# One-hot of slot numbers laid out contiguous per choice, slot number repeated along its columns, and the table of Silu loaded ahead

## The reference, cut to what matters

```python
x = x + tanh(g_xattn[0]) * sliding_window_attention(layernorm(x), ctx, ctx)
# layer 0: 32 experts, 8 a token, out of 4 of 8 groups
scores = sigmoid(flat @ gate_w.T)
topk_w, topk_i = group_topk(scores)
for e in range(32):
    h = silu(flat @ wg[e].T) * (flat @ wu[e].T)
    acc = acc + w[:, e] * (h @ wd[e].T)          # w is 0 where e isn't chosen
x = x + tanh(g_ffn[0]) * (acc + shared(flat))
x = x + tanh(g_xattn[1]) * cross_attention(layernorm(x), ctx)
# layer 1: 8 experts of 256, 2 a token, and two shared ones
x = x + tanh(g_ffn[1]) * moe1(layernorm(x))
```

## Time and profile before

| | us |
|---|---|
| median of 3 timed runs | 1098.48 |
| lowest, highest | 1097.58, 1100.46 |
| profiled execution | 1091.63 |
| its span | 1089.8 |

### The profile page before, as it was taken

How to read it: one execution, slowest core, us unless ns; L and a number is a source line. 1 busy time by engine, 2 the same in 40 slices (tenths; PEclk the granted TensorE clock), 3 DMA queues, 4 the chain that set the end, 5 groups by cost and what they waited for, 6 DMA issues and landing times.

```text
span 1089.8 us, 20602 instructions
## 1 busy us (share of the span) xinstructions
PE 929.6 (85%) x5529; PEld 716.2 (66%) x5529; DVE 690.3 (63%) x1965; ACT 441.1 (40%) x1030; POOL 544.2 (50%) x581
## 2 busy tenths in 40 slices
PE   3468888887699999999999926979999998999893
PEld 3357777776545888888888614655656564787672
DVE  5669999998674875555555247785857346444334
ACT  4558888893052444443444302122322313233230
POOL 7246655645003765555654477777700000787641
PEclk9769999998666999999999977989999997999997
DMA  8950000002101776776778647443300011466647
GB/s 244 226 121 2 1 0 0 0 2 94 59 1 40 221 219 204 217 224 209 221 202 150 229 149 258 128 140 111 111 1 20 1 58 26 86 109 133 134 81 245
DMA packets 75225, 127.44 MB, mean 117 GB/s; under 512 B 12480, under 2 KB 52032, under 8 KB 75008
## 3 DMA queue, kind: packets, MB, share of 16 engines
q0 software_dynamic: 21264, 48.02, 19.6%
q1 hardware_dynamic: 32240, 57.47, 17.4%
q10 hardware_dynamic: 21632, 20.85, 5.5%
HBM read 80.62 MB, written 36.77 MB: 108 GB/s over the span
## 4 chain that ended last, share of the span: by engine, by line
PE 57%; DVE 19%; DMA 7%; issue 7%; POOL 5%; ACT 2%; SPq 2%; DVEq 0%; ACTq 0%; POOLq 0%
PE bank L914 17%; PE bank L929 9%; PE bank L1600 5%; DVE ptl L618 4%; PE bank L903 4%; POOL yg L1193 4%; DMA sw<-in_w 3%; PE bank L810 3%; DVE nmax L610 3%; PE bank L922 2%; PE bank L424 2%; PE bank L1500 2%; PE bank L1535 2%; PE bank L1659 2%; PE bank L1560 2%
## 5 line engine op out<-in xcount | busy, mean ns | idle before, releaser
L1178 POOL DMA_INDIRECT xg<-token_rows,gather_idx x198 | 191.2, 966 | 215.2 <-PE bank L903 87.9
L914 PE MATMUL bank<-sw,xgt 128*128 x948 | 244.0, 380 | 0.4 <-issue 0.4
L914 PEld LDWEIGHTS bank<-sw,xgt 128*128 128x128 f32 x948 | 164.9, 190 | 15.2 <-issue 0.8
L1193 POOL DMA_INDIRECT yg<-slot_rows,slot_of x128 | 138.2, 1080 | 60.0 <-issue 33.8
L1007 ACT ACTIVATE ssil<-bank 128x128 f32<-128x128 f32 x237 | 65.7, 278 | 199.6 <-PE bank L914 199.5
L929 PE MATMUL bank<-sw,sht 128*128 x474 | 144.4, 387 | 0.1
L1099 DVE COPY xgt<-bank 128x256 f32<-128x256 f32 x198 | 83.9, 424 | 83.6 <-PE bank L903 76.0
L1112 DVE COPY sht<-bank 128x128 f32<-128x128 f32 x237 | 69.1, 292 | 105.8 <-PE bank L922 105.5
L546 ACT ACTIVATE prob<-bank,nmax 128x256 f32<-128x256 f32 x256 | 111.7, 511 | 8.1 <-DVE nmax L610 8.1
L424 PE MATMUL bank<-consts,prob 128*128 128x128 f32 x512 | 83.9, 289 | 35.2 <-DVE ptl L618 33.0
L610 DVE TENSOR_REDUCE nmax<-bank 128x2 f32<-128x512 f32 x128 | 87.7, 685 | 17.8 <-PE bank L411 17.3
(11 more groups left out here) (218 smaller groups left out, 1645.9 us busy)
## 6 DMA issues: line engine op xcount, KB each, us to landing
slot_rows<-ysb ACTq DMA_DIRECT2D x79, 256.0 KB, 3.4
sw<-in_w SPq DMA_DIRECT2D x48, 384.0 KB, 3.6
kst<-khl SPq DMA_DIRECT2D x32, 224.0 KB, 5.6
token_sums<-zeros SPq DMA_DIRECT2D x2, 2176.0 KB, 12.1
token_rows<-xn SPq DMA_DIRECT2D x8, 512.0 KB, 3.9
sums<-token_sums SPq DMA_DIRECT2D x8, 512.0 KB, 7.3
xg<-token_rows,gather_idx POOLq DMA_INDIRECT x198, 3.7
x<-in_x SPq DMA_DIRECT2D x4, 512.0 KB, 5.7
```

Of the source, the lines that this page charges most:

```text
L914: mm = pe.matmul(bank[2 + k % 2][:, 0:2 * FF], xgt[:, i % 3, c * P:(c + 1) * P], w[:, :, c, :], start=(c == 0), stop=(c == CH - 1))
L1178: nc.gpsimd.indirect_dma_start(xg[:, (first + i) % XG_RING, 0:ROW[L]], None, rows[L], bass.IndirectOffsetOnAxis(gather_idx[:, i:i + 1], 0) ...
L1193: nc.gpsimd.indirect_dma_start(yg[:, t % Y_TILES, j, :], None, ybuf[L], bass.IndirectOffsetOnAxis(slot_of[:, t, j:j + 1], 0)).then_inc(s_y ...
```

## The change

`hot_hi` becomes [128, 4, 8, 160]: the choice comes first and the blocks are contiguous, with rows of 160 of which 159 (or 39) are used. Both operands of the comparison are broadcast to [128, choices, blocks]: `iota_col`, now a single row of 159 numbers, along the choices, and `posh` along the blocks, so that one value is repeated for a whole row of outputs. `table` reads `hot_hi[:, t, j, 0:cols]` without a step. `hot_lo` and `hot_tok` stay as they are. GpSimd's iota for `iota_col` writes 159 values where it wrote 1272. Behind `hots_by_token` in layer 0 ScalarE gets one more activation, Silu of one column into `unread`, which nothing reads. A semaphore `hotp` is created and not used. Since `iota_col` is smaller and `hot_hi` a little larger, the buffers behind `iota_col` lie 2,208 bytes lower, those behind `hot_hi` 2,144.

```diff
-        iota_col = sb("iota_col", [P, BLOCKS[0], 8], F16)
+        iota_col = sb("iota_col", [P, BLOCKS[0]], F16)
+        unread = sb("unread", [P, 1], F32)
...
-        hot_hi = sb("hot_hi", [P, HOTS, BLOCKS[0], 8], F16, rt)
+        hot_hi = sb("hot_hi", [P, HOTS, 8, BLOCKS[0] + 1], F16, rt)
...
-                    mm = pe.matmul(bank[5][:, P:P + cols], hot_tok[:, t % HOTS, :, j], hot_hi[:, t % HOTS, 0:cols, j],
+                    mm = pe.matmul(bank[5][:, P:P + cols], hot_tok[:, t % HOTS, :, j], hot_hi[:, t % HOTS, j, 0:cols],
...
             hots_by_token(act, 0, m, range(TILES))
+            nc.scalar.activation(unread[:, :], tg[:, 0:1], ACT.Silu)
...
-                nc.gpsimd.iota(iota_col[:, :, :], [[1, BLOCKS[0]], [0, 8]], base=0, channel_multiplier=0,
+                nc.gpsimd.iota(iota_col[:, :], [[1, BLOCKS[0]]], base=0, channel_multiplier=0,
...
+        def hot_columns(ops, L, t):
+
+            top, cols = (TOP0, TOP1)[L], BLOCKS[L]
+            shape = [P, top, cols]
+            return ops.tensor_tensor(hot_hi[:, t % HOTS, 0:top, 0:cols], iota_col[:, 0:cols].unsqueeze(1).broadcast_to(shape),
+                                     posh[:, t, 0:top].unsqueeze(2).broadcast_to(shape), ALU.is_equal)
...
-                nc.vector.tensor_tensor(hot_lo[:, t % HOTS, :, 0:top], iota_lo[:, :, 0:top],
-                                        posl[:, t:t + 1, 0:top].broadcast_to([P, P, top]), ALU.is_equal)
-                op = nc.vector.tensor_tensor(hot_hi[:, t % HOTS, 0:cols, 0:top], iota_col[:, 0:cols, 0:top],
-                                             posh[:, t:t + 1, 0:top].broadcast_to([P, cols, top]), ALU.is_equal)
+                op = nc.vector.tensor_tensor(hot_lo[:, t % HOTS, :, 0:top], iota_lo[:, :, 0:top],
+                                             posl[:, t:t + 1, 0:top].broadcast_to([P, P, top]), ALU.is_equal)
+                if True:
+                    op = hot_columns(nc.vector, L, t)
                 op.then_inc(m.hot, 1)
...
-            nc.vector.tensor_scalar(started[0:ne, 0:cols], iota_col[0:ne, 0:cols, 0], incl[0:ne, 0:1], None,
+            nc.vector.tensor_scalar(started[0:ne, 0:cols], iota_col[0:ne, 0:cols], incl[0:ne, 0:1], None,
                                     ALU.is_ge).then_inc(m.bexp, 1)
```

More of the change, by code:

```diff
@@ L282, in gated_xattn_moe_kernel @@
             "hots": 16,
+            "hotp": 4,
             "hotf": 15,
@@ L317, in __init__ @@
                 self.hots = own["hots"]
+                self.hotp = own["hotp"]
                 self.hotf = own["hotf"]
```

## The result

| | before | after |
|---|---|---|
| median, us | 1099.88 (20 runs) | 1093.05 (20 runs) |
| lowest, highest | 1094.81, 1103.48 | 1085.72, 1101.91 |
| ratio after/before | | 0.9947 [0.9931, 0.9964] |
| profiled execution (span) | 1091.63 (1089.8) | 1095.98 (1094.1) |

The change makes the kernel 5.8 us faster, with an interval of 4.0 to 7.6 us (the ratio, which is taken over all the runs, times 1099.88; the medians differ by 6.8). The forecast was 1089.1 in a range of 1083 to 1096, and faster by over 0.3% with 0.86: the time is in the range and the direction is right, but the gain is 5.8 us and not 9.4. Note the last line of the table: of the two profiled executions the *changed* kernel's is the slower one, by 4.3 us. Whoever compares these two profiles by their totals gets the sign wrong, so they have to be compared by stages.

A forecast was written before the change was run, and what follows sets the result against it. The prediction took TensorE's strided matmuls in layer 0's `table` stage as the bound. Its terms, -4.9 - 2.0 - 1.9 - 0.8 + 0.2 = -9.4 us, taken off the 1098.5 median, gave 1089.1 us, range 1083 to 1096.

The forecast's parts named there:

- The bound and the swap: Layer 0's `table` stage: contiguous columns free TensorE from 288 ns a matmul, VectorE becomes the bound; -4.9 us.
- Rival 2: Layer 0's `table` stage: strided weights keep TensorE the bound at 288 ns; +0.7 in place of -4.9, 1094.7 us; chance 0.06.
- The price of `hot_hi`: VectorE in layer 0's `table` stage: the repeated slot number makes `hot_hi` last 1.48 us, a tile 2.01 us.
- The upper end of the bracket: Cost of `hot_hi` on VectorE: 1.04 ns a value, from 32-bit operations, against 0.50 at the lower end.
- rivals 1 (0.8 us): Layer 0's `hot_hi` keeps the 16-bit pace, 1.34 us a tile on VectorE; 1078.3 us; chance 0.08.
- 3 (over 2 us): Layer 0's repeated read is dearer, `hot_hi` 2.50 us; +11.4 in place of -4.9, 1105.4 us; chance 0.05.
- The iota: Last four normalisations: VectorE stands behind GpSimd's iotas, so 1113 values less give -2.0 us.
- The clock in the logits: Last two blocks' logits: a shorter TensorE wait may keep the clock up; ends 0 and -3.7, taken as -1.9 us.
- The early table of Silu: Start of layer 0's experts: loading Silu's table under ScalarE's idle returns TensorE's idle, -0.8 us, at most 1.28.
- Layer 1: Layer 1's `hot_hi` of 78 values takes 240 ns, 17 more than before, 12 times; +0.2 us (0 to 0.5).
- Rival 4: Whole kernel: buffers 2,208 bytes lower and shifted clock steps, a few tenths of a per cent either way; chance 0.05.
- The level: Start of the whole-kernel forecast: median of three timed runs, 1098.5 us; the profiled execution, 1091.6, would become 1082.2.

The follow-up runs named there:

- e4: Changed kernel with each slot number stored twice side by side in `posh`, `hot_hi` written as 80 pairs a row; 1083.18 us, ratio 0.9865 to the kernel before.
- e9: Changed kernel without the early Silu, with the old 1272-value iota added into an unread buffer ahead of the new one; 1091.55 us, ratio 0.9945 to before.
- after again: Changed kernel with no edit, profiled a second time; 1095.31 us in that profile.
- after third: Changed kernel with no edit, profiled a third time; 1090.85 us in that profile.
- e3: Changed kernel without the additional early Silu activation; 1095.49 us, ratio 0.996 to the kernel before.
- e2: Changed kernel with a GpSimd iota of 1113 running numbers into an unused buffer behind `iota_col`; 1090.21 us, ratio 0.9929 to the kernel before.

## Why the prediction was right, and where it was not

**The bound and the swap: right.** TensorE's 288 ns a matmul was the strided `hot_hi`; contiguous, 8 of them take 0.77 us at full clock (e4) and 1.29 at half, as forecast: (1.29 - 0.2) / 8 = 136 ns apart, with the 0.2 us for the end that the forecast also used. Rival 2, that the strided weights hold TensorE at 288 ns, is out. Layer 1's 77 ns in the earlier trace rows was the right witness.

**The price of `hot_hi`: right.** Forecast 1.48, measured 1.479 us; the tile 2.00 for 2.01; the stage from the cast to `gather_idx` 34.95 for 39.96, -5.0 for -4.9. The upper end of the bracket was the right end, and rivals 1 (0.8 us) and 3 (over 2 us) are out in the form in which they were stated. That the single repeated value is what costs, and not the rows, e4 shows. The Trainium skill ("Vector Engine (DVE) Microarchitecture Reference", section 5.1) had one element read 16 times as an input of a two-source operation with 2-byte operands at one result a cycle; the trace agrees, since 1272 / 0.96 = 1325 ns lies 154 under the 1479 measured, and 1280 at two a cycle, 667 ns, lies 159 under the 826 of e4.

**The iota: right.** -2.0 us forecast, 5.02 - 2.98 = 2.04 measured, returned whole by e9. VectorE does stand behind GpSimd: the first of the four `xn` takes 2.02 us beside an iota of 1.94 (row in the last section), where the earlier ones took 0.37.

**The clock in the logits: the term that failed first.** I had put half of 3.7 us on it (its own parts add to 3.8), with ends 0 and -3.7. It was 0 in the profiled run, -1.1 and -0.8 in the second and third, and +2.8 in two of the experiments' profiles: an end that my bracket didn't have. The step that failed reads "With the wait down to 1.1 us the clock may stay up". The wait went down to 2.23 us in the profiled execution, and to between 1.04 and 1.21, the forecast's value, where TensorE's first 16 transposes had taken 3.4 to 3.6 us (after again, after third, e3). There the eight last transposes did come faster, in 1.09 to 1.18 us in place of 1.97, which is most of the -1.1 and -0.8; but the last two blocks' 32 matmuls still took 6.60 to 6.88 us in every run without fillers. What my bracket lacked was that the iota's length was itself a cover: where the clock falls early, TensorE's slow logits used to lie under it. Over the six executions with the short iota and no fillers or added iota (9.42, 8.31, 8.63, 12.23, 8.58, 12.22) the mean is 9.90, so I estimate the term at about +0.5 and not -1.9. Six values between -1.1 and +2.8 don't fix it well; the changed kernel's own three give -0.6.

**The early table of Silu: the second.** The first Silu does come 1.3 us sooner (340.69 - 332.38 = 8.3 us behind the end of `gather_idx`, where it was 350.56 - 340.91 = 9.65), which is the load's 1.28 us. The Trainium skill ("ScalarE: Activation LUTs", What ACT_TABLE_LOAD costs) has 2.66 us with the drain; the traces do not show that much here. The load stands under ScalarE's idle as forecast. But "what returns is TensorE's idle: -0.8 us" was wrong: the idle moved to the gather of a later block, and the 41st Silu comes at the same distance. The step looked at the wait that was removed and, from 380 us on, at a stretch with no idle; between the two lie the first gathers, each 1.25 us behind the last. I had not asked there what would be late next.

**Layer 1: nothing.** `hot_hi` there went from 223 to 230 ns, not to 240; the term of +0.2 is not to be seen.

**The addresses: a term that was missing.** Rival 4 named them (2,208 bytes lower, "a few tenths of a per cent either way") and gave them 0.05 as a case of its own, and the sum had nothing for them. They cost 1.2 us, 0.1%, in the last loads, in every profile with the new addresses.

**The sum.** -5.0 - 2.0 + about 0.5 + 1.2 and 0 for the rest is -5.3 us; measured is -5.8 with an interval of -4.0 to -7.6. Against the forecast of -9.4 the clock accounts for 2.4 us, the last loads for 1.2, the Silu for 0.8. What is left, about 0.5 us, is within the uncertainty of the clock's term and of the runs. The `yg` sums took 104.1 us in the mean of three profiles before and 105.7 in the ten with the changed layout; with 3.6 us between profiles of one program that is not shown to be an effect of the change, and it stays open.

**The level.** Taking the sum off the median of the timed runs and not off the profiled execution was what kept the forecast in range: 1082.2 would have been 11 us off. The experiments show why: that profile had drawn low values in two stages that the change doesn't touch. As it is, the forecast lies 4.0 us below the measured time, 2.6 of them from the gain (9.4 against the 6.8 between the medians) and 1.4 from the median of three runs that it started from, 1098.5 where twenty gave 1099.9.

## What to carry to other kernels

When a layout makes a matmul's columns contiguous, look at what the engine that writes them pays for it: here 16 us of gain on TensorE became 5, since one input was a single repeated value, and doubling that value in memory brought the writer back to its old pace. Of a wait that is removed at the head of a stage, ask which transfer sets the next step before its gain is booked. And a stage that is slow may be the cover of another that is sometimes slow: look at it in more than one execution. Last, a buffer that shrinks moves all those behind it: compare also the stages that the change does not touch, as the loads at the end here.

## What the runs showed of the hardware

**Strided columns.** A matmul of 159 columns of 16 bits at a step of 16 bytes took 288 ns whatever the clock: in the trace of before the first ten started 0.29 us apart at a granted clock of 1.00, and the rest, at 0.50, did so too. Contiguous, 8 of them took 0.77 us at 1.00 and 1.29 at 0.50, or 71 and 136 ns each with the 0.2 us for the end taken off. So the strided form costs four times the contiguous one at the upper level and twice at the lower, and its price is not TensorE's own clock.

**Iota.** The same 1272 values cost 2.39 us as 159 numbers written 8 times each (e9), while 1113 running numbers cost 1.16 (e2): 1.9 against 1.0 ns a value.

**Where a load lands.** Eight loads of 512 KB into `sums` landed 1.36 us apart in the four profiles with the old addresses and 1.49 to 1.50 in the nine in which the buffer lay elsewhere, and the end of the kernel took 1.2 us more.

**VectorE and GpSimd in each other's way.** Both directions are in these traces. An `xn` lasts as long as the iota beside it, 2.02 us in place of 0.40; the first of the four in the changed kernel:

```profile
263.21 2.02 DVE L763 TENSOR_SCALAR xn<-x,meanvar,rstd 128x256 f32<-128x256 f32 x1 [1.47 <-POOL rstd L744]
```

And an indirect DMA's instruction on GpSimd, 0.95 us elsewhere, takes up to 5.23 us while VectorE adds the gathered rows:

```profile
673.89 6.41 DVE L1212 SCALAR_TENSOR_TENSOR x<-yg,gate_of,x 128x256 f32<-128x256 f32 x16
...
674.50 1.08 POOL L1197 DMA_INDIRECT yg<-slot_rows,slot_of  x1 [0.30 <-DVE x L1212]
675.88 5.23 POOL L1197 DMA_INDIRECT yg<-slot_rows,slot_of  x1 [0.31 <-DVE x L1212]
681.42 0.95 POOL L1197 DMA_INDIRECT yg<-slot_rows,slot_of  x1 [0.30 <-issue]
```

The gather ends at 681.11, 0.8 us behind the last of the 16 additions. In each of the 13 profiles four or five gathers of the `yg` stretch last over 1.3 us; by how much differs from one execution to the next, and the sums tend to be longer where they last longer, though not strictly. The Trainium skill ("SBUF — State Buffer", Who interferes with whom) has VectorE and GpSimd share one pair of ports under an exclusive lock, so that the loser is blocked and not slowed; the waits of `xn` for the whole iota agree. That the lock is also what holds the gathers was not tried here.
